# Experts' index chain one block deeper, fetch behind the transposition, and no mixer work for padding tiles

## The chip, the cores and the metric

The kernel runs on one core of a Trainium2 chip. The metric is the device time of one execution in microseconds; three runs of the kernel before have a median of 5204.59 us (5203.95 to 5213.59). A separate execution was recorded by the hardware profiler.

## The reference

One layer over 12500 nodes of 256 features. The rows are normalised (`xn`), pass two graph convolutions (a weighted sum over 212500 sorted edges, a 256x256 product, ELU) and, beside them, linear attention with 8 heads and an MLP (the mixer); the sum is `x2`. Then 8 experts, each row to its best one:

```
xn = layernorm(x)
x = x + gnn(xn, src, dst, edge_weight) + mix(xn)
h = layernorm(x)
idx = argmax(softmax(h @ gate_w + gate_b))
y = relu(h @ w1[idx] + b1[idx]) @ w2[idx] + b2[idx]
out = x + nan_to_num(y * prob)     # at most 1954 rows per expert
```

## The kernel before

`prepare` normalises. `gather` runs twice. One of its 104 turns takes 2048 edges: GpSimd issues 16 indirect gathers of 128 source rows (L448) into one of two buffers; VectorE makes 16 selection matrices (L402); TensorE multiplies rows and selections in 4 groups of 16 products (L394) into PSUM; VectorE adds the four windows to `agg` (L408). GpSimd may fill a buffer again when TensorE has begun the turn after. Two guests work in the same turns, called by place between the groups: the mixer, one tile of 128 nodes per turn (`keys_values` in the first gather, `attend` in the second), and the dense part 8 turns later, for nodes whose sums are complete (`dense_first`, `dense_second`; z product L595, L1211). There are 98 tiles of nodes (`UNITS`) and 104 turns (`TURNS`), so the mixer's tiles 98 to 103 are padding that nobody reads. `two_by_two` writes the first 12 turns out and loops over the rest. Behind the last turn the dense part finishes nodes 96 and 97 (`dve_end`, `act_end`, `pe_end`), on the same engines and in order behind the mixer's last tile.

`route` puts row numbers into slots, 8 experts with blocks of 256 slots. In `experts` every engine loops over the experts and over each one's blocks n:

- GpSimd (`block_of`): waits for the transposition, shifts `fetch_i` to `next_i` to `target_i` (`pass_on`), loads `fetch_i` for the new block, fetches its rows (`tokens`, L1731), and then handles an older block (`move`): gathers its rows of `x2` (L1739), waits for VectorE's result, scatters it to `out` (L1745), waits for the landing.
- TensorE: 32 hidden products of block n (L1804), the transposition of block n+1 (`turn`, L1793), 32 output products of block n (L1816).
- ScalarE and VectorE: relus (L1833, L1867), copy of the transposed rows (L1828).
- VectorE: `finish(n)` clamps the scaled output of the block before, replaces NaNs (L1848 to L1855) and adds `x2` (L1859); then bias (L1872) and probability (L1876) of block n.
- SyncE: when an expert's last block is scaled, loads the weights of the expert after next (L1426 to L1429).

Every order is that of the code; semaphores tie the engines.

Of the kernel before, what the change touches and what calls it, by code (L numbers as in the profile page):

```python
# [51 lines left out]
AGG = SPARE + WIN  # L52
TABLES = "natural_log_exp_and_others"
# [287 lines left out]
def gather(nc, m, layer, source, mixer, denser):  # L341
# [4 lines left out]
    with ExitStack() as ctx:  # L346
# [63 lines left out]
        with nc.Block(f"gather{layer}") as block:  # L410
            @block.sync
            def _(sp):
# [6 lines left out]
                def turn(i, u):  # L419
# [3 lines left out]
                    mix.free(sp, i - 1, u)  # L423
                    mix.load(sp, 2 * i + u, u)
                    mix.store(sp, i - 1, u)
# [5 lines left out]
                with sp.Fori(dense.peeled, loops) as i:  # L431
                    for u in range(2):
                        turn(i, u)
                mix.load_past(sp)
                for u in range(2):
                    dense.sp(sp, loops - 1, u)
                mix.stored(sp)
# [282 lines left out]
def keys_values(nc, m, sb, sem, ps, shared):  # L720
# [44 lines left out]
    def pe(pe, i, u, place):  # L765
        t = 2 * i + u
        if place == 0:
# [20 lines left out]
    def dve(dve, i, u, place):  # L788
        t = 2 * i + u
        if place == 1:  # L790
# [8 lines left out]
    def act(act, i, u, place):  # L799
        t = 2 * i + u  # L800
        if place:
            return
# [28 lines left out]
    mix.load_past = mix.stored = mix.dve_begin = mix.act_begin = mix.dve_end = mix.act_end = lambda engine: None  # L831
# [3 lines left out]
def attend(nc, m, sb, sem, ps, shared):  # L835
# [78 lines left out]
    def load_past(sp):  # L914

        free(sp, TURNS // 2 - 1, 0)
        load(sp, TURNS, 0)

    def all_stored(sp):
        for u in range(2):  # L920
            store(sp, TURNS // 2 - 1, u)

# [25 lines left out]
    def pe(pe, i, u, place):  # L948
        t = 2 * i + u
        if place == 1:  # L950
            pe.wait_ge(queries_ready, t + 1)
            for h in range(KD):
                last = nc.tensor.matmul(num_ps[:, h, :], queries[:, h, :], m.kv[:, h, :], start=True, stop=True)
            last.then_inc(num_ready, 1)
            if not before_first(i, u, 1):
                mlp_output(pe, t - 1)
        if place == 2:
# [4 lines left out]
            turn_tile(pe, t + 1, 1 - u, i + u)  # L962
# [4 lines left out]
        if place == 4:  # L967
# [4 lines left out]
            project_queries(pe, t + 1, 1 - u)  # L972
# [7 lines left out]

    def pe_end(pe):
        mlp_output(pe, TURNS - 1)
# [43 lines left out]

    def dve_begin(dve):
        min_query(dve, 0)

    def dve(dve, i, u, place):  # L1030
        t = 2 * i + u
        if place == 0:
# [4 lines left out]
        if place == 1:  # L1037
            dve.wait_ge(num_ready, t + 1)

            nc.vector.tensor_scalar(den[:, :, :], num_ps[:, :, P:KVW], ATT_EPS, 1.0 / N,  # L1040
                                    ALU.add, ALU.mult).then_inc(den_ready, 1)
            dve.wait_ge(den_ready, t + 1)
            nc.vector.reciprocal(inv[:, :, :], den[:, :, :]).then_inc(inv_ready, 1)
            dve.wait_ge(inv_ready, t + 1)
            nc.vector.tensor_tensor(msg[:, :].rearrange("p (k h d) -> p k h d", k=KD, h=HC),
                                    num_ps[:, :, 0:P].rearrange("p k (h d) -> p k h d", h=HC),
                                    inv[:, :, :].rearrange("p k (h o) -> p k h o", o=1)
                                    .to_broadcast([P, KD, HC, HD]), ALU.mult).then_inc(msg_ready, 1)
            if not before_first(i, u, 1):
                output_variance(dve, t - 1)  # L1050
        if place == 2:
            if not before_first(i, u, 1):
                output(dve, t - 1, 1 - u)
            dve.wait_ge(msg_projected, t + 1)
            variance(dve, t, 0)

            dve.wait_ge(result_free[u], i + 1)
            dve.sem_inc(m.passed, 1)
            nc.vector.tensor_tensor(result[:, u, :], tile[:, u, :], m.ln2_b[:, :], ALU.add).then_inc(base_ready, 1)
            inverse_sd(dve, t, 0)  # L1060
            normalise(dve, msg[:, :], 0).then_inc(normed_ready, 1)
# [937 lines left out]
```

## Time and profile before

| | |
|---|---|
| median of three runs | 5204.59 us |
| profiled execution, its own time | 5200.88 us |
| its span | 5199.2 us |
| busy | PE 80%, POOL 66%, DVE 51%, ACT 17% |
| clock of TensorE, mean | 0.863 |
| gather 1, gather 2, routing, experts begin at about | 180, 2276, 4448, 4546 us |

Times count from the span's start. A row of the timeline gives the start, the busy time, the engine and line, the operation with what it writes and reads, the count merged into the row, and in brackets how long the engine stood idle before it and what ended that. PE is TensorE, DVE VectorE, ACT ScalarE, POOL GpSimd, SPq SyncE's queue.

### The profile page before, as it was taken

To read this page: it belongs to the slowest core of one execution; us is meant where nothing else is said; L and a number is where in the kernel's file an instruction comes from. 1 tells how busy PE (TensorE), PEld (TensorE's weight loads), DVE (VectorE), ACT (ScalarE), POOL (GpSimd) and SP (SyncE) were. 2 spreads that over 40 slices of the span, in tenths; PEclk is the share of its full clock that TensorE was granted. 3 is DMA by queue.
4 is the path that set the end of the run, shared out by engine and by line. 5 is a ranking of instruction groups with operands and counts; after the bars stand their busy time and mean duration, and the time that the engine had idled before them with its cause. 6 is when DMAs were issued, how large, how long until landed. Compare 5 with 4: busy or idle time off the path is not lost. (4 is left out here: it accounts for less than half of the span.)

```text
span 5199.2 us, 89417 instructions
## 1 busy us (share of the span) xinstructions
PE 4146.8 (80%) x25462; PEld 3778.9 (73%) x25463; DVE 2677.2 (51%) x9521; ACT 870.8 (17%) x2703; POOL 3438.1 (66%) x3718
## 2 busy tenths in 40 slices
PE   0477777777777777758988889899899998689998
PEld 0467766666767776758888888888888888377776
DVE  7433333333333333355676676666666676634444
ACT  2001000010000000011222222222222222511111
POOL 0577777777777777757777777777777776044443
PEclk9867777777777777769999999999999999799999
DMA  7444444444444444434555544545545555122111
GB/s 213 131 116 118 118 118 118 118 118 118 118 118 118 118 118 118 118 85 119 147 149 148 152 146 144 153 145 146 153 144 148 148 147 147 47 86 67 66 66 65
DMA packets 363720, 641.03 MB, mean 123 GB/s; under 512 B 105821, under 2 KB 233053, under 8 KB 363533
## 3 DMA queue, kind: packets, MB, share of 16 engines
q0 software_dynamic: 171648, 468.64, 31.4%
q1 hardware_dynamic: 184357, 157.61, 9.8%
q10 hardware_dynamic: 7632, 13.77, 0.7%
q8 instruction: 42, 0.69, 0.1%
q14 instruction: 41, 0.34, 0.0%
HBM read 550.18 MB, written 89.52 MB: 123 GB/s over the span
## 5 line engine op out<-in xcount | busy, mean ns | idle before, releaser
L394 PEld LDWEIGHTS sums<-sel,rows 128*128 128x128 f32 x13312 | 1883.0, 221 | 768.4 <-DMA rows<-xn,idx 426.7
L394 PE MATMUL sums<-sel,rows 128*128 128x64 f32 x13312 | 1887.6, 304 | 674.2 <-DMA rows<-xn,idx 319.9
L448 POOL DMA_INDIRECT rows<-xn,idx x1664 | 1578.1, 948 | 642.9 <-issue 632.8
L448 POOL DMA_INDIRECT rows<-h,idx x1664 | 1586.9, 954 | 572.4 <-issue 524.4
L402 DVE TENSOR_SCALAR sel<-cols,rel_now,wgt_now 128x64 f32<-128x64 f32 x3360 | 779.5, 336 | 7.8
L408 DVE TENSOR_TENSOR agg<-agg,sums 128x128 f32 x832 | 240.1, 289 | 783.7 <-issue 615.3
L600 DVE TENSOR_TENSOR pre<-z,b_g 128x256 f32<-128x256 f32 x98 | 41.6, 424 | 530.7 <-PE z L595 530.7
L1816 PE MATMUL y_ps<-w,e_hidden 128*128 128x256 f32 x1248 | 286.6, 389 | 0.0
L1804 PE MATMUL e_hidden_ps<-tokens_t,w 128*128 128x256 f32 x1248 | 278.2, 381 | 0.9 <-ACT tokens_t L1828 0.9
L977 PE MATMUL hidden_ps<-xt,w 128*128 128x128 f32 x1664 | 265.5, 282 | 16.4 <-ACT msg_t L1098 16.2
L1816 PEld LDWEIGHTS y_ps<-w,e_hidden 128*128 128x128 f32 x1248 | 242.2, 197 | 33.3
L1804 PEld LDWEIGHTS e_hidden_ps<-tokens_t,w 128*128 128x128 f32 x1248 | 238.7, 191 | 34.2 <-ACT tokens_t L1828 1.3
L977 PE MATMUL hidden_ps<-msg_t,w 128*128 128x128 f32 x1664 | 254.3, 275 | 0.0
L977 PEld LDWEIGHTS hidden_ps<-xt,w 128*128 128x128 f32 x1664 | 221.1, 193 | 34.9 <-ACT msg_t L1098 34.9
L940 PE MATMUL row_ps<-w,hidden 128*128 128x256 f32 x832 | 228.5, 424 | 2.7 <-ACT hidden L1102 2.7
L977 PEld LDWEIGHTS hidden_ps<-msg_t,w 128*128 128x128 f32 x1664 | 220.0, 193 | 0.0
L776 PE MATMUL kv_proj<-w_k,kv_xt 128*128 128x256 f32 x416 | 209.7, 660 | 0.0
L1745 POOL DMA_INDIRECT out<-y_result,target_i x82 | 81.3, 991 | 190.5 <-DVE y_result L1859 175.8
L792 DVE TENSOR_SCALAR k_min<-kv_proj 128x256 f32<-128x256 f32 x104 | 44.1, 424 | 304.9 <-PE kv_proj L776 304.9
L940 PEld LDWEIGHTS row_ps<-w,hidden 128*128 128x128 f32 x832 | 174.2, 220 | 27.4 <-ACT hidden L1102 2.9
L965 PE MATMUL row_ps<-w_m,msg_t 128*128 128x256 f32 x416 | 124.4, 424 | 70.6 <-ACT msg_t L1090 70.6
L776 PE MATMUL kv_proj<-w_v,kv_xt 128*128 128x256 f32 x416 | 177.3, 575 | 0.0
(225 smaller groups left out, 4735.8 us busy)
## 6 DMA issues: line engine op xcount, KB each, us to landing
rows<-xn,idx POOLq DMA_INDIRECT x1664
rows<-h,idx POOLq DMA_INDIRECT x1664
w<-in_ffn_w SPq DMA_DIRECT2D x16, 1024.0 KB, 7.4
tile<-xn SPq DMA_DIRECT2D x105, 128.0 KB
ln_rows<-in_x SPq DMA_DIRECT2D x52, 256.0 KB
xn<-ln_normed ACTq DMA_DIRECT2D x52, 256.0 KB, 4.4
kv_tile<-xn SPq DMA_DIRECT2D x104, 128.0 KB
mix<-result SPq DMA_DIRECT2D x104, 128.0 KB
```

The source lines that it names most:

```text
L394: last = nc.tensor.matmul(sums[:, g, h, :], rows[:, u, k, h * P:(h + 1) * P], sel[:, u, k, :], start=(c == 0), stop=(c == GROUP - 1))
L402: last = nc.vector.tensor_scalar(sel[:, u, k, :], m.cols[:, :], rel_now[:, u, k:k + 1], wgt_now[:, u, k:k + 1], ALU.is_equal, ALU.mult)
L408: return nc.vector.tensor_tensor(window, window, sums[:, g, :, :], ALU.add)
L448: nc.gpsimd.indirect_dma_start(out=rows[:, u, k, :], out_offset=None, in_=source, in_offset=bass.IndirectOffsetOnAxis(ap=idx[:, u, k:k + 1 ...
L776: last = nc.tensor.matmul(proj[n][:, 0, :], xt[:, k, :], w[:, k, :], start=(k == 0), stop=(k == KD - 1))
L792: nc.vector.tensor_scalar(k_min[:, :], proj[0][:, 0, :], 0.0, None, ALU.min).then_inc(k_min_ready, 1)
L940: last = nc.tensor.matmul(row_ps[1], hidden[:, o, :], m.w_2[:, o, :], start=(o == 0), stop=(o == F1 // P - 1))
L965: last = nc.tensor.matmul(row_ps[0], msg_t[:, k, :], m.w_m[:, k, :], start=(k == 0), stop=(k == KD - 1))
L977: last = nc.tensor.matmul(hidden_ps[:, o, :], m.w_1[:, k, o * P:(o + 1) * P], of, start=(k == 0), stop=(k == 2 * KD - 1))
L1745: nc.gpsimd.indirect_dma_start(out=m.out, out_offset=bass.IndirectOffsetOnAxis(ap=target_i[:, tt:tt + 1], axis=0), in_=result[:, tt, :], i ...
L1804: last = nc.tensor.matmul(hidden_ps[f % HB], m.w1[u][:, k, f * P:(f + 1) * P], tokens_t[:, k, :], start=(k == 0), stop=(k == KD - 1))
L1816: last = nc.tensor.matmul(y_ps[tt], hidden[:, f, tt * P:(tt + 1) * P], m.w2[u][:, f, :], start=(f == 0), stop=(f == FC - 1))
```

## The change

In the experts GpSimd keeps one more set of indices (`last_i`). An iteration copies four index tiles, waits for the transposition, fetches, waits for the result of two blocks back, scatters it, gathers `x2` for the block after that one, and waits for all three to land. `out_free` is given after the scatter's landing and before the wait for `x2`; `finish` waits for one more of them. A further `move` follows at the end. `zeros` is set by VectorE.

In the gathers `has_tile` leaves the mixer's loads, stores, products and vector work out for tiles 98 to 103, and the last 8 turns are written out on all engines but GpSimd. The functions that finished tile 103 behind the turns are gone.

```diff
+LATE = (TURNS - UNITS) // 2 + 1
 def two_by_two(engine, loops, body, peeled=1):
...
-    with engine.Fori(peeled, loops) as i:
+    with engine.Fori(peeled, loops - LATE) as i:
         for u in range(2):
             body(i, u)
+    for i in range(loops - LATE, loops):
+        for u in range(2):
+            body(i, u)
+def has_tile(i, u, ahead=0):
+    return not isinstance(i, int) or 2 * i + u + ahead < UNITS
...
     def pe(pe, i, u, place):      # attend; act and dve alike
         t = 2 * i + u
         if place == 1:
-            pe.wait_ge(queries_ready, t + 1)
...
-            if not before_first(i, u, 1):
+            if has_tile(i, u):
+                pe.wait_ge(queries_ready, t + 1)
...
+            if not before_first(i, u, 1) and has_tile(i, u, -1):
                 mlp_output(pe, t - 1)
-        if place == 2:
+        if place == 2 and has_tile(i, u):
...
-    def pe_end(pe):
-        mlp_output(pe, TURNS - 1)
...
-                def pass_on(n):
+                def pass_on(n, of):
                     nc.gpsimd.tensor_copy(target_i[:, :], next_i[:, :]).then_inc(indices, 1)
-                    wait_apart(pool, indices, 3 * n + 1, m.pool_passed)
-                    nc.gpsimd.tensor_copy(next_i[:, :], fetch_i[:, :]).then_inc(indices, 1)
-                    wait_apart(pool, indices, 3 * n + 2, m.pool_passed)
+                    wait_apart(pool, indices, 4 * n + 1, m.pool_passed)
+                    nc.gpsimd.tensor_copy(next_i[:, :], last_i[:, :]).then_inc(indices, 1)
+                    wait_apart(pool, indices, 4 * n + 2, m.pool_passed)
+                    nc.gpsimd.tensor_copy(last_i[:, :], fetch_i[:, :]).then_inc(indices, 1)
+                    wait_apart(pool, indices, 4 * n + 3, m.pool_passed)
+                    nc.gpsimd.tensor_copy(fetch_i[:, :], of).then_inc(indices, 1)
+                    wait_apart(pool, indices, 4 * n + 4, m.pool_passed)
-                def fetch():
+                def fetch(n):
+                    wait_apart(pool, turned, n + 1, m.pool_passed)
                     for tt in range(TT):
...
                 def move(n):
-                    for tt in range(TT):
-                        nc.gpsimd.indirect_dma_start(
-                            out=x2[:, tt, :], out_offset=None, in_=m.x2,
-                            in_offset=bass.IndirectOffsetOnAxis(ap=target_i[:, tt:tt + 1], axis=0)
-                        ).then_inc(x2_gathered, 16)
                     wait_apart(pool, result_ready, n + 1, m.pool_passed)
                     for tt in range(TT):
...
+                    for tt in range(TT):
+                        nc.gpsimd.indirect_dma_start(
+                            out=x2[:, tt, :], out_offset=None, in_=m.x2,
+                            in_offset=bass.IndirectOffsetOnAxis(ap=next_i[:, tt:tt + 1], axis=0)
+                        ).then_inc(x2_gathered, 16)
                     pool.wait_ge(out_scattered, (n + 1) * (16 * TT))
                     pool.sem_inc(out_free, 1)
+                    wait_apart(pool, x2_gathered, (n + 1) * (16 * TT), m.pool_passed)
                 def block_of(e, u, ii, n, first):
-                    wait_apart(pool, turned, n + 1, m.pool_passed)
-                    pass_on(n)
...
-                    fetch()
+                    pass_on(n, slots_of(m.slot_i, e, n, first))
+                    fetch(n)
                     move(n)
+                    wait_apart(pool, tokens_loaded, (n + 1) * (16 * TT), m.pool_passed)
...
+                pass_on(end + 2, m.spare_i[:, 0:TT])
+                move(end + 2)
...
                 def finish(n):
-                    wait_apart(dve, out_free, n + 1, m.passed)
+                    wait_apart(dve, out_free, n + 2, m.passed)
...
-                nc.vector.memset(result[:, :, :], 0.0).then_inc(result_ready, 1)
+                nc.vector.memset(result[:, :, :], 0.0).then_inc(result_ready, 2)
```

GpSimd, one iteration over a block of an expert, before:

```order
L1724 COPY target_i<-next_i 128x2
L65 ISA
L1726 COPY next_i<-fetch_i 128x2
L65 REGISTER_ALU
L1754 ISA
L1754 COPY fetch_i<-slot_token 128x2
L65 REGISTER_ALU
L1731 DMA tokens<-xf,fetch_i 128x256 x2
L1739 DMA x_of_tokens<-x,target_i 128x256 x2
L1745 DMA out<-y_result,target_i 12544x256 x2
L1748 REGISTER_ALU
```

The same iteration after (names: `out` is the result's scatter, `x_of_tokens` the gather of x2):

```order
L1733 COPY target_i<-next_i 128x2
L66 ISA
L1735 COPY next_i<-last_i 128x2
L66 REGISTER_ALU
L1737 COPY last_i<-fetch_i 128x2
L66 REGISTER_ALU
L1739 ISA
L1739 COPY fetch_i<-slot_token 128x2
L66 REGISTER_ALU x2
L1745 DMA tokens<-xf,fetch_i 128x256 x2
L1754 DMA out<-y_result,target_i 12544x256 x2
L1758 DMA x_of_tokens<-x,next_i 128x256 x2
```

One copy more; the scatter stands ahead of the x2 gather, which goes by `next_i`.

TensorE, second gather, the end of the last turn and what follows it, before (`hidden_ps` and `row_ps` are the mixer's MLP, `z_xf` the dense part):

```order
L394 MATMUL sums<-sel,rows 128x64 x8
L1198 MATMUL num_ps<-gate_w,xf_t 128x8 x2
L1205 MATMUL z_xf<-ident,xf_rows 128x128 x2
...
L977 MATMUL hidden_ps<-xt,w 128x128 x2
L977 MATMUL hidden_ps<-msg_t,w 128x128 x2
L99 REGISTER_ALU
L99 COMPARE_AND_BRANCH
L940 MATMUL row_ps_2<-w,hidden 128x256 x4
L1198 MATMUL num_ps<-gate_w,xf_t 128x8 x2
L1205 MATMUL z_xf<-ident,xf_rows 128x128 x2
L1211 MATMUL z_xf<-w_g,agg_nodes 128x256 x2
```

The whole last turn and what follows it, after:

```order
L92 ISA x4
L403 MATMUL sums<-sel,rows 128x64 x24
L1205 MATMUL num_ps<-gate_w,xf_t 128x8 x2
L1212 MATMUL z_xf<-ident,xf_rows 128x128 x2
L1218 MATMUL z_xf<-w_g,agg_nodes 128x256 x2
L403 MATMUL sums<-sel,rows 128x64 x8
...
L1205 MATMUL num_ps<-gate_w,xf_t 128x8 x2
L1212 MATMUL z_xf<-ident,xf_rows 128x128 x2
L1218 MATMUL z_xf<-w_g,agg_nodes 128x256 x2
```

Between the last window products and the dense part's next z product nothing of the mixer is left; in the turn only the dense steps stand between the groups.

## Rows read from the trace of the kernel before

**Rows 1.** The experts' stretch: us, busy per engine, clock, DMA share, GB/s.
```profile
4557.01:5184.57 627.56, 578.23 (x2652) 498.11 (x2652) 268.61 (x581) 96.66 (x195) 256.54 (x352) 0.97 0.21 71
```

**Rows 2.** Timeline, TensorE in the experts: hidden products, and transpositions behind waits.
```profile
4557.01 9.53 PE L1804 MATMUL e_hidden_ps<-tokens_t,w 128*128 128x256 f32 x32 [0.91 <-ACT tokens_t L1828]
...
4610.81 7.07 PE L1804 MATMUL e_hidden_ps<-tokens_t,w 128*128 128x256 f32 x32
...
4625.06 7.07 PE L1804 MATMUL e_hidden_ps<-tokens_t,w 128*128 128x256 f32 x32
...
4796.63 7.07 PE L1804 MATMUL e_hidden_ps<-tokens_t,w 128*128 128x256 f32 x32
...
4825.13 1.12 PE L1793 MATMUL e_turn_ps<-ident,tokens 128*128 128x128 f32 x4 [2.68 <-DMA tokens<-xf,fetch_i]
```

**Rows 3.** Waits in the experts: us in total, times, longest.
```profile
PE e_turn_ps L1793 <- DMA tokens<-xf,fetch_i: 60.2, 28, 11.0
```

**Rows 4.** Timeline, GpSimd, one iteration in the experts and its successor's start.
```profile
4800.25 0.19 POOL L1724 COPY target_i<-next_i 128x2 int32<-128x2 int32 x1 [3.57 <-issue]
...
4802.20 1.01 POOL L1731 DMA_INDIRECT tokens<-xf,fetch_i  x1 [0.87 <-POOL fetch_i L1754]
4803.51 0.96 POOL L1731 DMA_INDIRECT tokens<-xf,fetch_i  x1 [0.30 <-issue]
...
4806.18 1.14 POOL L1739 DMA_INDIRECT x_of_tokens<-x,target_i  x1 [0.30 <-issue]
4810.63 1.00 POOL L1745 DMA_INDIRECT out<-y_result,target_i  x1 [3.31 <-DVE y_result L1859]
...
4814.92 0.18 POOL L1724 COPY target_i<-next_i 128x2 int32<-128x2 int32 x1 [2.00 <-DMA out<-y_result,target_i]
```

**Rows 5.** Timeline, VectorE's finishing beside that iteration.
```profile
4804.14 0.59 DVE L1848 TENSOR_SCALAR y_result<-y_scaled 128x512 f32<-128x512 f32 x1
...
4806.68 0.73 DVE L1855 COPY_PREDICATED y_result<-nan,y_zeros 128x512 f32<-128x512 uint8 x1
4809.09 0.69 DVE L1859 TENSOR_TENSOR y_result<-y_result,x_of_tokens 128x512 f32<-128x512 f32 x1 [1.67 <-DMA x_of_tokens<-x,target_i]
```

**Rows 6.** One expert's second weight load issued, and such loads' time to landing.
```profile
4817.24 0.42 SPq L1427 DMA_DIRECT2D w<-in_ffn_w  x1
...
DMA to landing us min/median/max: 7.3/8.1/8.4
```

**Rows 7.** Timeline, the end of the second gather, all engines.
```profile
4402.66 0.95 POOL L448 DMA_INDIRECT rows<-h,idx  x1 [0.30 <-issue]
...
4409.44 1.89 PE L394 MATMUL sums<-sel,rows 128*128 128x64 f32 x16
...
4414.05 0.41 DVE L1216 TENSOR_TENSOR pre<-z_xf,b_g 128x256 f32<-128x256 f32 x1
...
4419.02 1.56 DVE L408 TENSOR_TENSOR agg<-agg,sums 128x128 f32 x4 [3.58 <-issue]
...
4422.52 3.78 PE L940 MATMUL row_ps<-w,hidden 128*128 128x256 f32 x8 [2.74 <-ACT hidden L1102]
...
4427.66 0.39 ACT L1173 COPY agg_nodes<-agg 128x256 f32<-128x256 f32 x1
...
4431.72 0.41 DVE L1216 TENSOR_TENSOR pre<-z_xf,b_g 128x256 f32<-128x256 f32 x1
```

**Rows 8.** Timeline, GpSimd, the first of the last two scatters.
```profile
5192.58 1.00 POOL L1745 DMA_INDIRECT out<-y_result,target_i  x1 [3.29 <-DVE y_result L1859]
```

**Rows 9.** Timeline, the end of the first gather: last issue, third group, mixer, z product.
```profile
2243.39 0.95 POOL L448 DMA_INDIRECT rows<-xn,idx  x1 [0.30 <-issue]
...
2247.91 3.67 PE L394 MATMUL sums<-sel,rows 128*128 128x64 f32 x16 [2.36 <-DMA rows<-xn,idx]
2251.37 1.18 PE L782 MATMUL kv_total<-values,keys 128*128 128x129 f32 x4
2252.34 1.91 PE L595 MATMUL z<-w_g,agg_nodes 128*128 128x256 f32 x4
```

More of the change, by code:

```diff
@@ L430, in _ @@
                         turn(i, u)
-                with sp.Fori(dense.peeled, loops) as i:
+                with sp.Fori(dense.peeled, loops - LATE) as i:
                     for u in range(2):
                         turn(i, u)
-                mix.load_past(sp)
+                for i in range(loops - LATE, loops):
+                    for u in range(2):
+                        turn(i, u)
                 for u in range(2):
                     dense.sp(sp, loops - 1, u)
-                mix.stored(sp)
                 dense.sp_end(sp)
@@ L766, in pe @@
         t = 2 * i + u
+        if not has_tile(i, u):
+            return
         if place == 0:
@@ L789, in dve @@
         t = 2 * i + u
+        if not has_tile(i, u):
+            return
         if place == 1:
@@ L800, in act @@
         t = 2 * i + u
-        if place:
+        if place or not has_tile(i, u):
             return
@@ L912, in store @@
         sp.sem_inc(result_free[u], 1)
[L914 to L921, printed above, removed]
     def turn_tile(pe, t, u, i):
@@ L950, in pe @@
         if place == 1:
-            pe.wait_ge(queries_ready, t + 1)
-            for h in range(KD):
-                last = nc.tensor.matmul(num_ps[:, h, :], queries[:, h, :], m.kv[:, h, :], start=True, stop=True)
-            last.then_inc(num_ready, 1)
-            if not before_first(i, u, 1):
+            if has_tile(i, u):
+                pe.wait_ge(queries_ready, t + 1)
+                for h in range(KD):
+                    last = nc.tensor.matmul(num_ps[:, h, :], queries[:, h, :], m.kv[:, h, :], start=True, stop=True)
+                last.then_inc(num_ready, 1)
+            if not before_first(i, u, 1) and has_tile(i, u, -1):
                 mlp_output(pe, t - 1)
-        if place == 2:
+        if place == 2 and has_tile(i, u):
             pe.wait_ge(msg_ready, t + 1)
@@ L966, in pe @@
             last.then_inc(msg_projected, 1)
-        if place == 4:
+        if place == 4 and has_tile(i, u):
             pe.wait_ge(normed_ready, t + 1)
@@ L1031, in dve @@
         t = 2 * i + u
-        if place == 0:
+        if place == 0 and has_tile(i, u):
             dve.wait_ge(q_exp_ready, t + 1)
@@ L1037, in dve @@
         if place == 1:
[L1038 to L1049, printed above, removed]
+            if has_tile(i, u):
+                message(dve, t)
+            if not before_first(i, u, 1) and has_tile(i, u, -1):
                 output_variance(dve, t - 1)
         if place == 2:
-            if not before_first(i, u, 1):
+            if not before_first(i, u, 1) and has_tile(i, u, -1):
                 output(dve, t - 1, 1 - u)
[L1054 to L1061, printed above, removed]
-        if place == 3:
+            if has_tile(i, u):
+                dve.wait_ge(msg_projected, t + 1)
+                variance(dve, t, 0)
+                dve.wait_ge(result_free[u], i + 1)
+                dve.sem_inc(m.passed, 1)
+                nc.vector.tensor_tensor(result[:, u, :], tile[:, u, :], m.ln2_b[:, :], ALU.add).then_inc(base_ready, 1)
+                inverse_sd(dve, t, 0)
+                normalise(dve, msg[:, :], 0).then_inc(normed_ready, 1)
+        if place == 3 and has_tile(i, u, 1):
             min_query(dve, t + 1)
-    def dve_end(dve):
-        output_variance(dve, TURNS - 1)
-        output(dve, TURNS - 1, 1)
     def copy_tile(act, t, u):
@@ L1086, in act @@
         if place == 0:
-            if not before_first(i, u, 1):
+            if not before_first(i, u, 1) and has_tile(i, u, -1):
                 guess_sd(act, t - 1, 1)
-            act.wait_ge(msg_turned, t + 1)
-            nc.scalar.copy(msg_t[:, :, :], turn_ps[:, :, :]).then_inc(msg_t_ready, 1)
-            copy_tile(act, t + 1, 1 - u)
-        if place == 1:
+            if has_tile(i, u):
+                act.wait_ge(msg_turned, t + 1)
+                nc.scalar.copy(msg_t[:, :, :], turn_ps[:, :, :]).then_inc(msg_t_ready, 1)
+            if has_tile(i, u, 1):
+                copy_tile(act, t + 1, 1 - u)
+        if place == 1 and has_tile(i, u):
             guess_sd(act, t, 0)
-        if place == 2:
+        if place == 2 and has_tile(i, u):
             act.wait_ge(norm_turned, t + 1)
```

62 lines of the change are left out of this document (36 added, 26 removed).

## The prediction

> **What bounds the kernel now.** I read the stretches first, then one engine's rows at a time. The last eighth of the span is the experts: from the first hidden product at 4557.01 to the end of the last output product at 5184.57 are 627.56 us, for 39 blocks of 256 rows, with TensorE at 0.97 of its clock [rows 1]. The block that starts at 4610.81 and its successor at 4625.06 are 14.25 us apart, the shortest distance and one without a wait [rows 2]. 39 x 14.25 = 555.8, so 71.8 us of the stage are not products at full rate. The waits name the cause: the transposition waits 60.2 us for tokens, 28 times [rows 3]. About 2.5 us more go to the first block (9.53 against 7.07 us for its hidden products, [rows 2]) and the rest to products that run slower behind such a wait.
>
> Why tokens come late is read on GpSimd [rows 4]. In one iteration it copies indices (4800.25), fetches tokens (4802.20), gathers x2 (second issue 4806.18), then stands still until VectorE has added x2 (4809.09, 0.69 long, [rows 5]), scatters from 4810.63, and starts its next copies at 4814.92. That is 14.67 us with no slack in it, because landing, addition, scatter and landing stand in a row; each expert boundary adds to it (the 3.57 us gap ahead of 4800.25, against 2.00 ahead of 4814.92). A chain of 14.7 and more cannot feed a block of 14.25.
>
> One second cause: a fetch issued while the next expert's weights come in lands when they land. The second weight load goes out at 4817.24, and such a load lands after 8.1 us: 4825.3; the transposition began at 4825.13, after 2.68 us of waiting [rows 2, 6].
>
> In the gathers GpSimd sets the pace: it issues one gather of 0.95 us each 1.25 us and waits only for its own issue [rows 7]. Work of the mixer there is hidden, except behind the last rows.
>
> **The change, experts.** The pending result is one block older, so the scatter no longer waits for an addition that waits for a gather of the same iteration. GpSimd's iteration becomes: four copies instead of three, 1.95 (4800.25 to 4802.20) + 0.35 = 2.3 to the first issue [rows 4]; six issues, each 1.30 apart (4802.20 to 4803.51), 7.5 to the end of the last; landing and turning round 2.0 (the gap ahead of 4814.92). Sum 11.8, and 1.6 more at a boundary (3.57 - 2.00): 13.4. Both are under 14.25.
>
> The added waits. The fetch waits for the transposition of the block before; behind it on GpSimd stand both scatters, both x2 gathers and the next copies. TensorE transposes 6.9 us into a block, so the fetch is issued from about 8 to 11 us and its tokens are wanted 21 us in: a whole block of cover. VectorE's finishing of a block now waits for the following iteration's scatter to land; behind it in VectorE's queue stand the two bias additions, the scaling and the next relus. The finishing starts 7.5 us into a block (4804.14 against 4796.63, [rows 2, 5]) and takes 4.2 (4804.14 to the end of the masks at 4807.4, and 0.69 for the addition). Result at 11.8; scatter from 12.6 (0.85 from result to issue: 4809.78 to 4810.63, [rows 4, 5]); x2 until 17.5; released at about 17.7, landed at 19.4, that is 5.1 us into the next block. It is asked for at 7.5, so 2.4 us are to spare each block. The loop result, scatter, gather, release, finishing is 0.85 + 5.1 + 0.2 + 4.2 = 10.4 us, also under 14.25. TensorE is late next, with its own products.
>
> So the stage costs 39 x 14.25 = 555.8, + 2.5 for the first block, + 5 for one wait at the start: GpSimd has no slack built up when expert 0 ends after two blocks, and its third or fourth fetch falls into the weight load, as at 4825.13. Bounds of that last term: 0 (the fetch goes out ahead of the load) and 15 (the first three loads each catch one). Sum 563.3, a gain of 64.3. Following all four engines block by block with these durations gives 624.0 for the kernel before, where the trace has 627.6: the way of counting leaves 3.6 us out, and may leave as much out after.
>
> The end of the stage gets longer. Before, the last output product ends at 5184.57, the last pair of scatters begins at 5192.58 [rows 8], and 14.6 us pass to the span's end. After: the last result waits for release 3.4 us past the end of the products (17.7 - 14.25), masks 3.3, addition 0.9, 0.85 to the issue, scatters 2.3, then a pair of x2 gathers nobody reads, 2.55, and from the last issue to the end 4.3 as before (5192.58 + 2.3 = 5194.9 to 5199.2). Sum 17.6: 3 us lost (0 to 6). The zeroing that GpSimd gives to VectorE is exchanged for two copies: nothing.
>
> **The change, padding tiles.** Turns 98 to 103 lose the mixer. GpSimd paces those turns, so the TensorE, VectorE and ScalarE work removed there is worth nothing until the last rows have landed.
>
> Second gather. The last gather ends at 4403.6. Its rows land by 4409.2 at the latest, when TensorE used them without waiting [rows 7]; in the first gather the last rows were used 3.57 us after their issue ended (2243.39 + 0.95 = 2244.34 to 2247.91, [rows 9]), so I take 4407.2. From there: third group of window products, gate, transposition and z product, then VectorE takes z (before at 4414.05) and 5.0 us later begins the window additions at 4419.02. Before, the group took 1.89 and the three dense steps 2.7 (4414.05 - 4409.44 - 1.89). I take 3.6 for the group, as in the first gather behind a wait (3.67, [rows 9]), and 3.3 for the steps, whose z product alone takes 1.91 there: z is there at 4414.1, so no gain up to the additions. After them the gain is certain: before, ScalarE copies the nodes for the next dense tile only at 4427.66, because the last padding tile's output product (4422.52, 3.78 long), its statistics and its guess stand ahead on each queue. After, the copy follows the additions' end (4420.6) by 0.4: 4421.0. From copy to z taken are 2.5 us (0.4 copy, 1.9 product, 0.2 handing over) instead of 4.06 (4427.66 to 4431.72), since VectorE does the residual ahead of it meanwhile. z is taken at 4423.5 instead of 4431.72: gain 8.2. The chain behind it is unchanged.
>
> The clock decides the rest. The same 16 products take 3.67 us behind the wait at 2247.91 and 1.89 at 4409.44 [rows 7, 9]: lower and upper level. With fewer products in these turns TensorE waits more, so I take the lower; at the upper z would come some 3 us sooner and the gain be 11. The Trainium skill, TensorE: Matmul & The Clock Gate, "What's actually happening", says that the throttled rate is the default and activity releases it; by that rule the padding work kept the clock up and part of its removal is given back, as the rows have it.
>
> First gather. The four products of keys and values (2251.37 to the z product at 2252.34: 1.0 us) leave the path between the last rows and z: gain 1.0, 0 to 1.5.
>
> The last eight turns are also written out instead of looped, on all engines but GpSimd, whose loop stays; 1.25 us an issue hides it. Price if instructions came late: each turn beyond 20 us; nothing in the first turns, written out too, shows it, so 0, at worst 5.
>
> Sum: 64.3 - 3 + 8.2 + 1.0 = 70.5 us. The profiled execution took 5200.88 (span 5199.2); the three timed runs have a median of 5204.59, 3.7 above. 5204.6 - 70.5 = 5134.
>
> **A rule against it.** GpSimd's issues beside VectorE's finishing are longer: 1.14 us at 4806.18, 0.95 in the gathers [rows 4, 7]. Six of them at +0.19 are 1.1 us, within the 2.4 spare. The Trainium skill, SBUF — State Buffer, "Who interferes with whom", says that VectorE's two-port forms shut GpSimd out of a shared port for a whole instruction. If scatters and gathers were each held for one mask operation (0.73 us, [rows 5]), four would add 2.9: 0.5 over the spare, 39 x 0.5 = 20 us, 5154.
>
> **Rivals.**
> 1. GpSimd's chain still binds, by such stays or by slower landing: 15 us a block instead of 14.25, about 29 us less gain, 5163; with 20 us less, 5154. For it: gaps of GpSimd vary, some issues have 2 us ahead of them. Against: 2.4 us to spare. 14%.
> 2. The padding part gives nothing, or is eaten by a slower clock and new code: 9 us less, 5143. 8%.
> 3. Slower: x2 gathers behind scatters land late. Each iteration now waits for both before its next fetch; with a landing of 6 us, as beside the weight loads, the sum is 2.3 + 7.5 + 6 + 0.3 = 16.1, equal to the 627.56 / 39 = 16.1 of before; it decides from there. At 7 us a block is 17.1: 39 us lost, 3 at the end, 9 won in the gathers: 5237. For it: 6 us do occur beside 2 MB of weights. Against: all other landings are about 2 us. 4%.
> 4. The chain doesn't come loose: a dependence I overlooked keeps 16.1 us, leaving 9 - 3 = 6 us: 5199. 4%.
>
> The forecast has 70%. Its own range, from the unknown terms (start 0 to 15, clock, end, the 3.6 left out), is 5124 to 5150. To hold 8 in 10 I take the nearer part of rival 1: 5122 to 5160. A difference under 0.2% is about 10 us, the spread of the three runs: rival 4 is "same" with 4%; slower 4%; faster 92%.
>
> **What would show it.** Waits of the transposition for tokens near zero but for one or two among the first blocks; blocks 14.25 us apart; scatters no longer preceded by 3 us for VectorE on the path, the copies followed by a wait for the transposition; 563 us from first hidden to last output product; 17 to 18 us behind it; copy of nodes about 0.4 us behind the last window additions. It is wrong if block starts are 15 us or more apart, or if GpSimd reaches its fetch after the transposition it waits for, block after block.

## The result, and the profile after

The changed kernel takes 5135.22 us (median of 4 runs, 5132.12 to 5136.85) beside 5204.27 (median of 4, 5203.67 to 5213.59): ratio 0.987, 95% interval 0.9858 to 0.9882. The forecast was 5134. Timed again in two of the groups below, it took 5132.49 and 5134.66.

| us, of the profiled executions | before | after |
|---|---|---|
| own time (span) | 5200.88 (5199.2) | 5136.3 (5134.5) |
| start to first hidden product of the experts | 4557.01 | 4552.46 |
| first hidden to end of last output product | 627.56 | 564.11 |
| from there to the end of the span | 14.6 | 17.9 |

The three lines differ by -4.55, -63.45 and +3.3, in sum by the 64.7 of the spans.

The experts' stretch, as in [rows 1] (us; busy time of PE, PEld, DVE, ACT, POOL; clock; DMA share; GB/s):

```profile
4552.46:5116.57 564.11, 560.20 (x2652) 491.99 (x2652) 266.69 (x581) 96.67 (x195) 291.72 (x398) 0.99 0.24 79
```

TensorE is busy for 560 of 564 us. Its timeline, the third block first, and an undisturbed block later (start, us, engine, line, operation; in brackets the wait and what ended it), to compare with [rows 2]:

```profile
4584.19 7.07 PE L1816 MATMUL e_hidden_ps<-tokens_t,w 128*128 128x256 f32 x32
4594.32 1.12 PE L1805 MATMUL e_turn_ps<-ident,tokens 128*128 128x128 f32 x4 [3.06 <-DMA tokens<-xf,fetch_i]
4595.23 8.26 PE L1828 MATMUL y_ps<-w,e_hidden 128*128 128x256 f32 x32
...
4646.08 7.07 PE L1816 MATMUL e_hidden_ps<-tokens_t,w 128*128 128x256 f32 x32
4652.99 0.60 PE L1805 MATMUL e_turn_ps<-ident,tokens 128*128 128x128 f32 x4
4653.42 7.07 PE L1828 MATMUL y_ps<-w,e_hidden 128*128 128x256 f32 x32
4660.33 7.07 PE L1816 MATMUL e_hidden_ps<-tokens_t,w 128*128 128x256 f32 x32
```

Blocks are 14.25 us apart (4646.08 to 4660.33). Inside the stage two waits for tokens are left, the 3.06 us above and 0.85 in the first block (us in total, times, longest):

```profile
PE e_turn_ps L1805 <- DMA tokens<-xf,fetch_i: 3.9, 2, 3.1
```

The same stretch before, from 4557.01 on, has

```profile
PE e_turn_ps L1793 <- DMA tokens<-xf,fetch_i: 49.1, 27, 3.5
```

The 60.2 of [rows 3] also hold the wait of 11.03 us ahead of the very first transposition, which lies before the stage begins and is there after the change too (10.97):

```profile
4554.98 1.12 PE L1793 MATMUL e_turn_ps<-ident,tokens 128*128 128x128 f32 x4 [11.03 <-DMA tokens<-xf,fetch_i]
```

One iteration of GpSimd, to be laid beside [rows 4]: fetch, scatter and gather follow one another at the pace of issue, and nothing for VectorE stands between.

```profile
4814.48 0.97 POOL L1745 DMA_INDIRECT tokens<-xf,fetch_i  x1 [0.99 <-POOL fetch_i L1739]
...
4817.02 1.00 POOL L1754 DMA_INDIRECT out<-y_result,target_i  x1 [0.30 <-issue]
...
4820.91 0.97 POOL L1758 DMA_INDIRECT x_of_tokens<-x,next_i  x1 [0.30 <-DMA out<-y_result,target_i]
4824.15 0.18 POOL L1733 COPY target_i<-next_i 128x2 int32<-128x2 int32 x1 [2.27 <-DMA x_of_tokens<-x,next_i]
...
4827.00 0.97 POOL L1745 DMA_INDIRECT tokens<-xf,fetch_i  x1 [0.98 <-POOL fetch_i L1739]
```

The end of the second gather, against [rows 7]:

```profile
4407.87 1.36 POOL L460 DMA_INDIRECT rows<-h,idx  x1 [0.30 <-issue]
...
4412.58 3.67 PE L403 MATMUL sums<-sel,rows 128*128 128x64 f32 x16 [1.59 <-DMA rows<-h,idx]
...
4419.28 0.42 DVE L1223 TENSOR_TENSOR pre<-z_xf,b_g 128x256 f32<-128x256 f32 x1 [9.44 <-PE z_xf L1218]
...
4423.57 1.56 DVE L417 TENSOR_TENSOR agg<-agg,sums 128x128 f32 x4 [3.04 <-issue]
...
4425.81 0.40 ACT L1180 COPY agg_nodes<-agg 128x256 f32<-128x256 f32 x1 [5.39 <-DVEq L517]
...
4428.38 0.42 DVE L1223 TENSOR_TENSOR pre<-z_xf,b_g 128x256 f32<-128x256 f32 x1 [0.20 <-PE z_xf L1218]
```

From the last issue's end to z taken are 19.15 us (4409.23 to 4428.38) instead of 28.11. But GpSimd's last issue ends 5.6 us later than before (4409.23 against 4403.61), so z is taken only 3.3 us earlier. Where those 5.6 us come from was the main open question of this trace.

### The profile page after: what moved, and what is told of

It reads as the page before. It is cut to its first block and busy times, and to the rows that moved or that the text cites. A ratio compares the mean times of both kernels' runs of the same rounds, so it can differ in the third digit from the quotient of the medians.

```text
span 5134.5 us, 87736 instructions
## 1 busy us (share of the span) xinstructions
PE 4113.3 (80%) x24996; PEld 3765.1 (73%) x24997; DVE 2643.0 (51%) x9389; ACT 846.1 (16%) x2617; POOL 3474.6 (68%) x3768
## 5 line engine op out<-in xcount | busy, mean ns | idle before, releaser
L403 PEld LDWEIGHTS sums<-sel,rows 128*128 128x128 f32 x13312 | 1939.0, 227 | 782.7 <-DMA rows<-xn,idx 414.2
L403 PE MATMUL sums<-sel,rows 128*128 128x64 f32 x13312 | 1944.8, 310 | 688.9 <-DMA rows<-xn,idx 312.1
L987 PE MATMUL hidden_ps<-xt,w 128*128 128x128 f32 x1568 | 250.1, 282 | 21.2 <-ACT msg_t L1108 21.0
L987 PE MATMUL hidden_ps<-msg_t,w 128*128 128x128 f32 x1568 | 239.4, 275 | 0.0
L987 PEld LDWEIGHTS hidden_ps<-xt,w 128*128 128x128 f32 x1568 | 208.3, 193 | 38.6 <-ACT msg_t L1108 38.6
L947 PE MATMUL row_ps<-w,hidden 128*128 128x256 f32 x784 | 215.9, 426 | 0.0
L987 PEld LDWEIGHTS hidden_ps<-msg_t,w 128*128 128x128 f32 x1568 | 207.1, 192 | 0.0
L790 PE MATMUL kv_proj<-w_k,kv_xt 128*128 128x256 f32 x392 | 198.0, 661 | 0.0
L790 PE MATMUL kv_proj<-w_v,kv_xt 128*128 128x256 f32 x392 | 164.7, 567 | 0.0
L1014 ACT ACTIVATE ln_var<-var 128x1 f32<-128x1 f32 x196 | 39.7, 203 | 729.1 <-DVE var L996 729.1
```

The source lines that it names most:

```text
L403: last = nc.tensor.matmul(sums[:, g, h, :], rows[:, u, k, h * P:(h + 1) * P], sel[:, u, k, :], start=(c == 0), stop=(c == GROUP - 1))
L790: last = nc.tensor.matmul(proj[n][:, 0, :], xt[:, k, :], w[:, k, :], start=(k == 0), stop=(k == KD - 1))
L947: last = nc.tensor.matmul(row_ps[1], hidden[:, o, :], m.w_2[:, o, :], start=(o == 0), stop=(o == F1 // P - 1))
L987: last = nc.tensor.matmul(hidden_ps[:, o, :], m.w_1[:, k, o * P:(o + 1) * P], of, start=(k == 0), stop=(k == 2 * KD - 1))
```

## The experiments

Theory: the deeper chain in the experts makes some 61 us, the padding part some 9, and in the experts only the depth counts. Rivals: the order of wait and copies counts as well; the padding part is worth less, or nothing, because the written-out turns or the clock take it back. Four kernels were timed together at a time, beside the kernel before.

**e1_after_again.** The changed kernel, unaltered.

> The changed kernel once more, unaltered, as the yardstick of this group and as a second profile of it. By the prediction's terms: 5134 us beside 5204 of the kernel before (64.3 - 3 in the experts, 9.2 in the gathers). By the first trace of it, in which the second gather's last issue ended 5.6 us later than before, the gain ahead of the experts is 4.5 us only; if that belongs to the change, the median stays above the kernel before minus 66; if it was one execution's pauses, this profile has its last issue elsewhere and the median stays near 5135.

5132.49 us, ratio 0.9869 (0.9854 to 0.9884).

**e2_experts_only.** Edit: both gathers as before, the function of the experts as after.

```
 mixers, gather, two_by_two: as before
-def experts: as before
+def experts: as after
```

> The kernel before with the changed experts alone: both gathers as before. Theory (the prediction's terms): 64.3 less from the first hidden to the last output product, 3 more behind it: 61.3 us, 5204.3 - 61.3 = 5143; first hidden to last output product 564. Rival, that a part of the experts' gain comes from entering the stage earlier or from the gathers: 55 us or less, 5149 and above.

5141.56 us beside 5202.1: 60.5 less; ratio 0.9883 (0.9868 to 0.9898). First hidden to last output product 563.73. The gain of 61.3 that the theory gave holds to within a microsecond.

**e3_padding_only.** Edit: the reverse, gathers as after, experts as before.

```
 mixers, gather, two_by_two: as after
-def experts: as after
+def experts: as before
```

> The kernel before with the changed gathers alone: padding tiles skipped, last eight turns written out, experts as before. Theory (the prediction's terms): 9.2 us less, 5195. Rival 1, from the first trace of the changed kernel (the end of the gather quicker by 9, but the last issue 5.6 us later because TensorE is at its lower level in the padding turns and GpSimd waits for it): 3 to 5 us less, 5200. Rival 2, eaten altogether: 5204.

5194.63 us beside 5202.1; ratio 0.9988 (0.9979 to 0.9997), that is 1.6 to 10.9 us less. It rules out rival 2 only barely, and cannot part 9 from 4. Nor can it be put down to the padding work alone: e4, timed in the same group, keeps that work and has the same interval. On top of the changed experts the same gathers are worth 9.1 us: the four runs of e1 (5131.59 to 5137.0) all lie below the four of e2 (5140.03 to 5146.5).

**e4_unrolled_only, e10_unrolled_again.** Edit to the kernel before (SyncE's loop likewise):

```
-    with engine.Fori(peeled, loops) as i:
+    with engine.Fori(peeled, loops - LATE) as i:
         for u in range(2):
             body(i, u)
+    for i in range(loops - LATE, loops):
+        for u in range(2):
+            body(i, u)
```

> The kernel before with the last eight turns of each gather written out instead of looped, the padding tiles still computed. Theory (the prediction put no price on it): 5204, within 2 us, clock in the padding turns 1.0 as before and the last issue where it was. Rival (code comes late): 5206 to 5209, with GpSimd's last issue of the second gather some 5 us later, as in the first trace of the changed kernel.

> The kernel before with the last eight turns of each gather written out, once more: its first timing came out 7 us below the kernel before although its profile shows no stage that gains by it, and 1.9 us lost where the written-out turns begin. If that was chance of the one chip: 5200 to 5206. If writing out does gain: 5195 again.

First 5195.0 beside 5202.1 (ratio 0.9979 to 0.9997), then 5200.09 beside 5202.12 (0.9983 to 1.0001). The 7 us are not found again, so most of them were chance: neither a gain nor a loss from writing out is shown.

The traces of all these kernels, cut by turns, divide the 5.6 us. The numbers are times between starts of GpSimd's issues in the second gather, 16 to a turn (turns counted from 0; the last ones up to the end of the last issue), and the stretch from there to the experts' first hidden product:

| us | turns 0, 1 | 2 to 95 | 96, 97 | 98 to 103 | last issue to experts |
|---|---|---|---|---|---|
| before | 49.89 | 1916.42 | 40.23 | 120.62 | 153.40 |
| e2 (gathers of before) | 52.49 | 1915.22 | 40.65 | 127.52 | 149.96 |
| e4 (written out) | 49.89 | 1917.90 | 42.09 | 121.65 | 150.25 |
| e10 (the same) | 52.95 | 1916.02 | 44.75 | 120.39 | 149.81 |
| after | 52.87 | 1916.60 | 42.10 | 121.83 | 143.23 |
| e1 (the same) | 49.85 | 1916.54 | 42.58 | 122.12 | 143.03 |
| e9 (the same) | 49.78 | 1914.58 | 44.96 | 122.14 | 143.85 |
| e3 (gathers of after) | 54.00 | 1922.99 | 41.55 | 121.82 | 142.59 |

- Turns 0 and 1 take 49.7 to 49.9 or 52.5 to 54.0, each in kernels with the same gathers. The difference is one pause ahead of turn 2, which half of the fourteen traces have: chance, 3.0 of the 5.6.
- Turns 96 and 97 take 40.2 and 40.7 us in the two traces where they are looped, and 41.1 to 45.0 in the twelve where they are written out (e5 to e8, e11 and e12 included); 1.9 more in the trace of after than in before. It is not shown that this is a price of writing out. The time is a pause at the first issues of turn 97, and in all kernels most pauses of this gather stand at such a place in every sixth turn: 25, 31, 37 and so on to 91, all looped, with 97 the next. Turn 91 alone pauses for 0.5 to 4.8 us beyond the usual 0.30 an issue, turn 97 for none and 0.5 where it is looped and 0.8 to 4.6 where it is written out. Turns 91 and 97 of after, then turn 91 of before:

```profile
4145.96 0.94 POOL L460 DMA_INDIRECT rows<-h,idx  x1 [1.88 <-issue]
...
4268.48 0.94 POOL L460 DMA_INDIRECT rows<-h,idx  x1 [1.88 <-issue]
```

```profile
4140.14 0.95 POOL L448 DMA_INDIRECT rows<-h,idx  x1 [3.56 <-issue]
4142.96 0.94 POOL L448 DMA_INDIRECT rows<-h,idx  x1 [1.88 <-issue]
```

- Turns 98 to 103 take 1.2 us longer without the padding work (121.8 to 122.1) than in before; e2 and e4 have 6.4 and 1.5 us of pauses between GpSimd's issues there, and without them 121.2 and 120.1. After, e1, e3 and e9 have no pause there at all, so GpSimd does not wait for a slower TensorE, as rival 1 of e3 had it. Its issues themselves are longer, 92.9 us in sum instead of 91.7: the last one of turns 100 to 103 takes 1.35, 1.23, 1.70 and 1.36 us in after, and 0.95 in before. In after each of them stands beside the dense part's additions on VectorE:

```profile
4387.12 1.70 POOL L460 DMA_INDIRECT rows<-h,idx  x1 [0.30 <-issue]
4387.24 0.41 DVE L1229 SCALAR_TENSOR_TENSOR mix_in<-pre,mix_in 128x256 f32<-128x256 f32 x1
4387.58 0.41 DVE L1233 SCALAR_TENSOR_TENSOR exps<-exps,x_in 128x256 f32<-128x256 f32 x1
4388.03 0.43 DVE L1238 TENSOR_TENSOR x_now<-mix_in,exps 128x256 f32<-128x256 f32 x1
```

- Behind the last issue the changed gathers win 6 to 11 us in every pairing.

The rest of the 5.6 is small: the gather starts 0.6 us earlier, and turns 2 to 95 take 0.2 longer.

**e5_chain_only.** Edit to the changed kernel: the wait ahead of the copies again.

```
 def fetch(n):
-    wait_apart(pool, turned, n + 1, m.pool_passed)
     ...
 def block_of(e, u, ii, n, first):
+    wait_apart(pool, turned, n + 1, m.pool_passed)
     pass_on(n, slots_of(m.slot_i, e, n, first))
     ...
```

> The changed kernel, but GpSimd waits for the transposition ahead of its four copies again, instead of behind them; the chain stays one block deeper. Theory (the depth makes the gain): the copies, 2.3 us, come after the transposition, the iteration of some 13 us still ends before the next transposition, the tokens still land 6 us before they are wanted: 5135, at most 5 us more for the first blocks. Rival (both halves are needed): the 2.3 us stand in each block's chain, 1 to 2 us a block are lost, 5175 to 5215.

5138.29 us; first hidden to last output product 563.95. The depth alone makes the stage's gain (564.11 in after).

**e6_wait_only.** Edit to the changed kernel, whose gathers stay: the experts' chain of before, with its wait moved behind three copies. Shown against the experts of before:

```
 def block_of(e, u, ii, n, first):
-    wait_apart(pool, turned, n + 1, m.pool_passed)
     pass_on(n)
     ...
+    wait_apart(pool, turned, n + 1, m.pool_passed)
     fetch()
     move(n)
+    wait_apart(pool, tokens_loaded, (n + 1) * (16 * TT), m.pool_passed)
```

> The changed kernel, but with the experts' chain as deep as before: x2 gathered ahead of the scatter of the same iteration, the result waited for in between; only the wait for the transposition is moved behind the three copies. Theory (the depth makes the gain; before, GpSimd stood still for VectorE's addition and the scatter's landing, not for the transposition): the experts take what they took before, the whole 5195 to 5200. Rival (the order of wait and copies matters): 1 to 2 us a block less, 5120 to 5160.

5198.69 us beside 5203.18, first hidden to last output product 629.51: what before had, and 2 us more. The two longest waits of GpSimd there show why: it stands still for the result and for the scatter, not for the transposition.

```profile
POOL out L1753 <- DVE y_result L1867: 168.5, 39, 9.2
POOL target_i L1731 <- DMA out<-y_result,target_i: 62.8, 31, 2.1
```

**e7_filler_1us, e8_filler_4us.** Edit to the changed kernel, at the end of each iteration, with K = 3 and K = 12:

```
+for k in range(K):
+    nc.gpsimd.tensor_copy(filler[:, :], fetch_i[:, :]).then_inc(filled, 1)
+    wait_apart(pool, filled, n * K + (k + 1), m.pool_passed)
```

> The changed kernel with three more small copies on GpSimd at the end of every iteration, each 0.18 us and 0.17 to the next: 1.05 us a block (up to 2 where they run beside VectorE's finishing). It measures the slack of GpSimd's chain. The prediction's slack, 2.4 us a block: no change, 5135. Rival, from the first trace of the changed kernel (free iterations are 12.4 to 13.4 us, one in each expert is 1.3 longer and one 3.9 longer; waits for TensorE and VectorE above the usual sum to some 15 to 20 us, 0.45 a block): (1.05 - 0.45) x 39 = 23 us longer, 5158.

> The same with twelve copies: 4.2 us a block. The prediction's slack of 2.4: (4.2 - 2.4) x 39 = 70 us longer, 5205. Slack of 0.45: (4.2 - 0.45) x 39 = 146 us longer, 5281. If the stage were not bound by GpSimd even then (tokens a whole block ahead): 5135.

5148.62 and 5246.15 us; first hidden to last output product 573.13 (+9.0) and 677.29 (+113.2). Both times lie between those that the two slacks gave. In e8 (groups: busy us, mean ns, idle before) the twelve copies of 34 iterations cost 91.7 us and 61.5 between them, and with 0.17 behind the last that is 4.7 a block; the transposition waits again:

```profile
L1774 POOL COPY filler<-fetch_i 128x2 int32<-128x2 int32 x408 | 91.7, 225 | 130.0 <-DMA x_of_tokens<-x,next_i 68.5 <-POOL filler L1774 61.5
```

```profile
PE e_turn_ps L1810 <- DMA tokens<-xf,fetch_i: 81.9, 34, 5.6
```

A block then takes (677.29 - 2.5) / 39 = 17.3 us, so GpSimd's own iteration is 17.3 - 4.7 = 12.6 us on average, boundaries included. The slack is 1.65 us a block, between the 2.4 of the prediction and the 0.45 that I had read from the waits; both of my numbers missed.

e7 does not give a second measure of it. Its three copies are 1.7 us a block (45.7 us for those of 39 iterations, 12.8 between them, 0.17 behind the last), as much as the average slack. But the 9.0 us stand in seven blocks, 1.0 to 1.9 us in each, and all others are 14.25 us long as without filler. The slack is not even, and a small filler shows only where it runs out first.

**e9_after_third.** The changed kernel, unaltered.

> The changed kernel unaltered, once more, as the yardstick of this group: 5132 to 5136. Its third profile also counts against the two readings of the second gather: by the traces so far the written-out turns cost about 1.9 us where they begin (turns 96 and 97 take GpSimd 42.1 instead of 40.2) and the turns behind 1.2 to 1.5, whereas the first two turns take 49.8 or 52.9 by chance in any kernel.

5134.66 us, ratio 0.9871 (0.9856 to 0.9886). Turns 96 and 97 took 44.96, more than expected, and 98 to 103 122.14.

**e11_late_short.** Edit to the changed kernel: hold back the weights, leave out the last x2 gathers.

```
 ...
 wait_apart(sp, y_scaled, (end + 1) * TT, m.sp_passed)
+wait_apart(sp, turned, end + 3, m.sp_passed)
 load_expert(sp, m, 2 * ii + (2 + u), u)
 ...
-move(end + 2)
+move(end + 2, more=False)
```

> The changed kernel with two terms of the forecast taken away: the load of an expert's weights is held back until the transposition of the block that runs then (so that no fetch which is wanted in the same block falls into it), and the last pair of x2 gathers, which nobody reads, is left out. Theory: the wait of 3.06 us for tokens at the third block and the slow products behind it go, 5 us, first hidden to last output product 559 instead of 564; behind the last product 15.4 instead of 17.9; 7.5 us less than the changed kernel in all, 5126 to 5128. Rival: the held-back load makes another fetch late, later in the block: 564 or more, only the 2.5 are won. Rival for the end: the last scatters' landing is what the end waits for, and the gathers behind them hide it: 17.9 as before.

5133.51 us, not parted from the 5134.66 of e9. Two opposite things happened. Behind the last product there are 14.81 us instead of 17.7 (e9): the useless gathers did cost 2.9. The stage took 565.59 instead of 564.11: the wait for tokens is gone, and the next expert but one waits for its own weights instead, with slow products behind it:

```profile
4602.78 9.93 PE L1818 MATMUL e_hidden_ps<-tokens_t,w 128*128 128x256 f32 x32 [3.50 <-DMA b<-in_ffn_b]
```

The load, held back from 4585.60 to 4592.62, is wanted by about 4599 and lands at 4602.8, so the 5 us, or somewhat more, are paid to one or the other. That the fetch was late because of the load is shown; that it can be had for nothing is not.

**e12_late_short_warm.** Edit to e11: products into a bank nobody reads, in the mixer's place (28 at each of two places a turn).

```
+if place in (1, 2) and not has_tile(i, u):
     ...
+    for r in range(7):
+        for o in range(F1 // P):
+            nc.tensor.matmul(hidden_ps[:, o, :], m.w_1[:, 0, o * P:(o + 1) * P], xt[:, u, 0, :],
+                             start=True, stop=True)
```

> The same, and TensorE given 56 products of 128x128 a turn that nobody reads in the six padding turns of the second gather, in place of the mixer's. It tests that the lower level of the clock there is what its missing work costs. Theory: granted clock 0.9 and above in the padding turns instead of 0.50, the last group of window products 1.9 us instead of 3.67, the gate, transposition and z product 2.0 instead of 3.3, from the last issue's end to z taken 16.5 instead of 19.1: 2.5 us less than the kernel without, and GpSimd's last six turns 120.6 instead of 121.8, 1.2 more. Rival: the products themselves stand ahead of the last window products and cost what the clock gives: no difference, or 3 us more.

5184.6 us, 51 more than e11. The dose was wrong: each place shows 56 instructions where I had counted 28, and takes 6.5 to 8.8 us.

```profile
4358.59 3.65 PE L403 MATMUL sums<-sel,rows 128*128 128x64 f32 x16 [4.82 <-DVEq L517]
4362.04 8.84 PE L962 MATMUL hidden_ps<-xt,w 128*128 128x128 f32 x56
4370.72 1.90 PE L403 MATMUL sums<-sel,rows 128*128 128x64 f32 x16
4372.45 6.47 PE L962 MATMUL hidden_ps<-xt,w 128*128 128x128 f32 x56
4378.76 1.90 PE L403 MATMUL sums<-sel,rows 128*128 128x64 f32 x16
```

TensorE became the bound of those turns (155.15 us for turns 98 to 103, and 163.9 instead of 143 from the last issue to the experts). The clock did rise: the granted clock of turns 100 to 103 is 0.85, where after has 0.50, and the second and third group take 1.90, while the first, behind a wait of 4.8 us, still takes 3.65. What a fitting dose would give stays open.

## Why the prediction was right, and where its terms were off

**Experts: 563.3 forecast, 564.11 measured.** Block distance, first block and the one early wait are as predicted. The last was put at 5: the block from 4584.19 to the next start at 4603.32 (4595.23 + 8.26 less the overlap of 0.17) is 19.13, 4.9 over 14.25. Its cause was named too: that fetch goes out at 4585.84 to 4588, 0.2 us behind the first half of the weight load, and lands when the load does; e11 moves the load and the wait goes with it. The 3.6 us that the counting left out before were not left out after.

What the prediction read wrong there, without harm to the sum, is how the 71.8 us that were lost before divide. Waits for tokens were 49.1 of them, not 60.2, and the products that run slower behind such a wait a good deal more than the 9 us that its account leaves for them. TensorE's 2652 instructions of the stage took 578.23 us before and take 560.20 after. So of the 63.45 us won, 45.4 are waiting and 18.0 are products that are no longer slow.

**Tail: 17.6 forecast, 17.9 measured**, and 14.8 without the last gathers, 3 less, where the sum's parts had 2.55.

**GpSimd's slack: 2.4 forecast, 1.65 measured.** The iteration was put at 11.8. It is 12.5 in the rows above: 7.4 for the issues (7.5 put down), 2.27 for landing (2.0), and 2.85 from the first copy to the first issue (2.3). The missed half microsecond is in the copies, the last two of which take 0.24 and 0.58 beside VectorE's finishing instead of 0.18. (The finishing, put at 4.2, is 4.0 by the rows that the prediction cites.) This margin was what kept rival 1 from happening: with 1.7 us more on GpSimd a block (e7), 9 us of the gain go.

One sign that the prediction had set for being wrong did come: in two thirds of the stage's blocks GpSimd reaches its fetch after the transposition that it waits for, most of them 1.5 to 5.1 us after its end, and in the other 13 it waits:

```profile
POOL tokens L1745 <- POOL fetch_i L1739: 25.6, 26, 1.0
POOL tokens L1745 <- PE e_turn_ps L1805: 17.6, 13, 1.6
```

It costs nothing, because of the cover that the prediction had worked out itself: these tokens are wanted by the next transposition, a block of 14.25 us later. The sign was too strict.

Of the lock that rival 1 feared the trace shows a part: beside VectorE's finishing one fetch takes 1.37 and 1.41 us,

```profile
4682.92 1.37 POOL L1745 DMA_INDIRECT tokens<-xf,fetch_i  x1 [1.14 <-PE e_turn_ps L1805]
4684.60 1.41 POOL L1745 DMA_INDIRECT tokens<-xf,fetch_i  x1 [0.30 <-issue]
```

against 0.97 alone: 0.4 each, not a whole mask operation of 0.73. No issue of the stage is longer than 1.41, and none of the 51 that stand beside no VectorE operation is longer than 1.01; but 11 of the 38 beside a masked copy take 0.97 all the same. The Trainium skill, SBUF — State Buffer, "Who interferes with whom", has the two lock a shared pair of ports against each other; the trace agrees that they interfere, and shows at most 0.44 us an issue in the experts (0.75 in the second gather, the 1.70 above).

**Second gather: 8.2 forecast, 3.3 in the trace (4.55 to the first hidden product).** The way from the last issue to z taken is right: 19.9 forecast (4403.6 to 4423.5), 19.15 measured, with rows used 3.35 us behind the issue's end (3.6), the group at 3.67 (3.6 taken), and the copy of nodes 0.7 behind the additions (0.4). The step that failed stands ahead of it: the prediction took GpSimd's pace through the padding turns as unchanged, and put what their missing work does there at 0. They take 1.2 us longer, by issues that are longer themselves. That is all of the shortfall that belongs to the change for certain. Of the rest of the lag of 5.6 us, 3.0 are the pause ahead of turn 2, which is chance, and 1.9 the pause at turn 97. Writing out, put at 0 with 5 at worst, may have a part in the latter; the pauses of the looped turns are as long, so no price is shown. In the first gather turns 96 and 97 take 40.0 to 40.3 in all kernels.

Set against that, the profiled execution of before was slow behind its last issue, 153.4 where e2, e4 and e10, with the same work, need 150. A like-for-like figure is 150 - 143 = 7 won behind the last issue and 1.2 lost ahead of it, and turn 97 is open. The timings allow this and the forecast: 9.1 by e1 and e2, 1.6 to 10.9 by e3. They do not part padding work from writing out.

**The clock** did what the prediction chose to assume: from turn 100 on the granted clock in the trace of after is 0.50, the lower of the two levels (1.2 and 2.4 GHz), where before had 1.00 in the stretch shown. After (columns as in the first row above):

```profile
4340.00:4360.00 20.00, 17.03 (x74) 16.32 (x74) 8.08 (x33) 1.69 (x6) 15.28 (x16) 0.50 0.46 136
```

Before:

```profile
4340.00:4360.00 20.00, 17.97 (x142) 16.96 (x142) 13.91 (x53) 4.74 (x17) 15.12 (x17) 1.00 0.53 149
```

TensorE runs half as many instructions there (74 against 142) and is still busy for 17 of 20 us. By the Trainium skill, TensorE: Matmul & The Clock Gate, "What's actually happening", the throttled rate is the default that activity lifts. The traces agree: fewer instructions went with the lower level, and the added products of e12 with 0.85.

**First gather: 1.0 forecast, 0.6 measured, for another reason than I gave.** The second gather's first issue comes at 2275.83 instead of 2276.45. The four products of keys and values are gone, but the z product takes 2.02 instead of 1.91 and the next group 3.51 instead of 2.07, at the lower clock. From the first gather's last issue to the second's first are 32.1 and 31.8 us with the loop of before (before, e2), 31.07 and 31.04 with the turns written out and the products kept (e4, e10), 30.9 to 31.5 in all the kernels without them. So what is won here came with writing out, as far as two traces with the loop can tell.

**Median against profile.** The sum of the terms was 70.5, the medians differ by 69.05 (e1: 69.6), the profiles by 64.6. The difference is the two executions profiled: before's was 3.4 below its median, after's 1.1 above. So the second gather's shortfall of 5 us and this offset are largely the same thing, the chance of the two executions profiled, such as the pause ahead of turn 2 in after alone. By the medians only 1.5 us are missing. That the terms of the gathers come out so near is partly luck, since no timing shows them one by one; the experts' 61 are not, since e2 has them alone.

## What to carry to other kernels

When an engine's iteration holds a transfer, an addition that needs it and a second transfer that needs the sum, one more buffered stage takes the two landings out of the row; what matters is the depth, and the order of waits inside the iteration may be worth nothing (e5, e6). After such a change measure the slack with a filler that is large enough for the engine to pace every block (e8): counting rows and adding up waits both missed, and a small filler showed only the blocks where slack runs out first (e7). And judge a gain of a few microseconds stage by stage over several profiles: the same code moved by 3 us ahead of one turn and by 3 us behind its last issue. Before a pause at the place of an edit is called its price, look whether the same pause stands where nothing was edited.

## What was not expected of the hardware

- In the second gather, and only there, GpSimd's issues pause: apart from the usual 0.30 us, the gaps sum to 17 to 27 us over turns 2 to 95 in all kernels (the pause ahead of turn 2 left out), and 55 to 87% of that stands in every sixth turn from 25 to 91, many of the pauses exactly 1.88 us. In the first gather there is none in the same turns. The cause was not tried.
- Where VectorE has no padding work, the last issue of turns 100 to 103 takes 1.14 to 1.70 us instead of 0.95 (after, e1, e3). In after it stands beside the dense part's additions each time. Overlap alone does not explain it: in before an issue beside the first two of these additions, at 4387.45, takes 0.95. No run was made on it.
